# Turning the second activations of a quantised layer by DMA instead of on TensorE

## The reference

```python
def _act_quant(a):
    scale = QB / jnp.clip(jnp.max(jnp.abs(a), axis=-1, keepdims=True), 1e-05)
    return jnp.clip(jnp.round(a * scale), -QB, QB) / scale      # QB = 127
def _bitlinear(x, w):
    return jnp.einsum('bsd,od->bso', _act_quant(x), _weight_quant(w))
h = _rmsnorm(layernorm(x), norm_w)
value, gate = jnp.split(_bitlinear(h, w_gv), 2, axis=-1)        # 512 -> 2 x 2048
h = _bitlinear(value * jax.nn.silu(gate), w_out)                # 2048 -> 512
x = x + residual + h
```

## Time and profile before

| | |
|---|---|
| median of three executions | 1015.0 us |
| profiled execution, its time and span | 1013.59 us, 1011.6 us |
| TensorE busy, granted clock | 994.7 us (98%), 0.997 |
| VectorE, ScalarE, GpSimd busy | 676.1, 634.0, 354.8 us |
| quantised layer's tiles, first expand to last contract | about 238 to 437 us |

### The profile page before, as it was taken

The page is one execution under the profiler, slowest core; times in us unless marked ns, Lnnn a source line. Parts: engine busy times, 40 slices in busy tenths (PEclk is TensorE's granted clock), DMA queues, the critical chain, the costliest instruction groups (busy, mean ns, idle before and its releaser), DMA issues.

```text
span 1011.6 us, 15863 instructions
## 1 busy us (share of the span) xinstructions
PE 994.7 (98%) x5515; PEld 783.6 (77%) x5538; DVE 676.1 (67%) x1211; ACT 634.0 (63%) x950; POOL 354.8 (35%) x516
## 2 busy tenths in 40 slices
PE   9999999999999999999999999999999999999996
PEld 6887888886455555577877877888888999999996
DVE  6757555538999998768675755578625566666662
ACT  6776788746888899887666556121214466666662
POOL 1023222114655554146455445000100244445542
PEclk9999999999999999999999999999999999999998
DMA  6693666630200100121222333302053688888863
GB/s 233 246 332 117 180 185 193 178 87 22 85 22 23 30 24 1 48 78 42 84 84 84 136 115 99 115 1 84 14 197 117 224 242 228 226 229 252 243 155 46
DMA packets 48673, 128.96 MB, mean 127 GB/s; under 512 B 6368, under 2 KB 6368, under 8 KB 47840
## 3 DMA queue, kind: packets, MB, share of 16 engines
q1 hardware_dynamic: 37584, 99.54, 29.7%
q0 software_dynamic: 10448, 27.53, 11.8%
q10 hardware_dynamic: 576, 1.05, 0.3%
HBM read 99.79 MB, written 28.31 MB: 127 GB/s over the span
## 4 chain that ended last, share of the span: by engine, by line
PE 68%; DVE 2%; ACT 1%; issue 1%; POOL 1%; DVEq 0%; ACTq 0%; POOLq 0%
PE bank L60 16%; PE bank L61 16%; PE bank L62 16%; PE bank L1641 9%; PE bank L1662 5%; PE bank L2571 1%; PE bank L1653 1%; PE bank L1671 1%; PE bank L1737 1%; PE bank L1715 0%; PE bank L1716 0%; PE bank L2558 0%; PE bank L2541 0%; PE bank L1747 0%; PE bank L1748 0%
## 5 line engine op out<-in xcount | busy, mean ns | idle before, releaser
L1641 PE MATMUL bank<-w,f_qT 128*128 128x512 bf16 x496 | 115.9, 379 | 1.9 <-DVE f_h L1932 0.8
L2391 POOL DMA_INDIRECT out<-e_y,scatter_idx x32 | 69.0, 2157 | 109.5 <-ACT e_y L2500 89.6
L2374 POOL DMA_INDIRECT e_xg<-xn_rows,gather_idx x32 | 32.1, 1003 | 162.4 <-DVE gather_idx L2779 96.8
L1641 PEld LDWEIGHTS bank<-w,f_qT 128*128 128x128 bf16 x512 | 48.6, 98 | 51.6 <-issue 1.2
L2431 ACT ACTIVATE s_m_h<-s_mid 128x512 fp32r<-128x512 f32 (+1 forms) x24 | 15.2, 632 | 101.1 <-DVE s_mid L2789 55.2
L2898 DVE TENSOR_TENSOR e_mid<-bank,e_sil 128x256 f32<-128x256 f32 (+1 forms) x47 | 19.7, 420 | 59.2 <-ACT e_sil L2470 59.2
L1662 PE MATMUL bank<-w,f_q2T 128*128 128x512 bf16 x249 | 57.5, 379 | 1.2 <-ACT f_q2T L1324 0.8
L1932 DVE SCALAR_TENSOR_TENSOR f_h<-bank,f_columns,f_sg 128x512 f32<-128x512 f32 x64 | 47.9, 748 | 11.5 <-PE bank L1641 6.1
L60 PE MATMUL bank<-e_xT_h,e_wg_h 128*128 128x256 f32 (+1 forms) x192 | 55.1, 287 | 0.0
L61 PE MATMUL bank<-e_xT_l,e_wu_h 128*128 128x256 f32 (+1 forms) x192 | 54.1, 282 | 0.0
L62 PE MATMUL bank<-e_xT_h,e_wu_l 128*128 128x256 f32 (+1 forms) x192 | 54.0, 281 | 0.0
(11 more groups left out here) (481 smaller groups left out, 3274.9 us busy)
## 6 DMA issues: line engine op xcount, KB each, us to landing
wraw<-in_wffn SPq DMA_DIRECT2D x48, 512.0 KB, 4.2
e_raw_g<-in_ew_gate SPq DMA_DIRECT2D x16, 704.0 KB, 4.2
e_raw_u<-in_ew_up SPq DMA_DIRECT2D x16, 704.0 KB, 5.7
e_raw_d<-in_ew_down SPq DMA_DIRECT2D x16, 512.0 KB, 6.5
sorted_y<-e_y SPq DMA_DIRECT2D x19, 256.0 KB, 4.1
x_rows<-rows SPq DMA_DIRECT2D x16, 256.0 KB, 2.0
xn_rows<-a_work SPq DMA_DIRECT2D x16, 256.0 KB, 2.0
s_raw<-x_rows SPq DMA_DIRECT2D x16, 256.0 KB, 2.8
```

The costliest lines, as they stand in the source:

```text
L1641: ins = pe.matmul(bank[c % 2][:, :], qT[t % 2][:, k * P:(k + 1) * P], w_gv(k, col + c * 512), start=(k == 0), stop=(k == KD - 1))
L2374: gp.indirect_dma_start(xg[t][u][:, :], None, g.xn_dram, bass.IndirectOffsetOnAxis(g.gather_idx[:, slot:slot + 1], 0)).then_inc(e_arrived[ ...
L2391: gp.indirect_dma_start(io["out"], bass.IndirectOffsetOnAxis(g.scatter_idx[:, slot:slot + 1], 0), e_y[t][u][:, :], None, compute_op=ALU.ad ...
```

## The change

SyncE turns q2 with one transposing DMA per tile, SBUF to SBUF (128 x 2048 in bf16, 512 KB), for tiles 0 to 14, and with two of half the width for tile 15. TensorE's turn_q2, ScalarE's copy_q2T and the semaphores q2T_ready and q2T_copied are gone; contract waits for q2T_in, and for tile 15's second half for q2T_last. low moves from VectorE to ScalarE, ahead of high, for the tiles 1 to 14. low and high wait for the DMA of the tile before, which reads q2. On SyncE, renewed, the Wq, router and bias loads and turn_q2(0) now come before the summaries; the Wg load is behind turn_q2(14), the halves of tile 15 behind the Wg load. In TensorE's tail turn_x(14) comes before contract(15).

```diff
-        vbank, gbank, tbank, obank, sbank = g.bank[0:2], g.bank[2:4], [x[:, :].bitcast(bf16) for x in g.bank[4:6]], g.bank[6], g.bank[7]
+        vbank, gbank, obank, sbank = g.bank[0:2], g.bank[2:4], g.bank[6], g.bank[7]
         sbank_b = sbank[:, :].bitcast(bf16)
...
+                def turn_q2(t):
+                    sp.wait_ge(q2_low, t + 1)
+                    sp.wait_ge(q2_high, t + 1)
+                    if t:
+                        sp.wait_ge(o_ready, t)
+                    sp.dma_start(q2T[:, :].rearrange("p (k n) -> p k n", n=P), q2[:, :], transpose=True).then_inc(q2T_in, 16)
+
+                def turn_q2_half(n):
+                    sp.wait_ge((q2_low, q2_high)[n], TT)
+                    if n == 0:
+                        sp.wait_ge(o_ready, TT - 1)
+                    sp.dma_start(q2T[:, half(n)].rearrange("p (k n) -> p k n", n=P), q2[:, half(n)], transpose=True).then_inc((q2T_in, q2T_last)[n], 16)
+
                 sp.dma_start(norm_b[:, :], io["norm_w"][0, :].partition_broadcast(P)).then_inc(norm_in, 16)
-                for part, (ready, mine) in enumerate(((summ_hi, c_summ_h), (summ_lo, c_summ_l))):
-                    sp.wait_ge(ready, 1)
-                    sp.dma_start(g.summ_dram[B - 1, part, :, :], f(mine[:, :])).then_inc(summ_out, 16)
                 sp.wait_ge(renewed, 1)
...
                 sp.dma_start(bg_raw[:, :], io["bg"]).then_inc(bias_in, 16)
+                turn_q2(0)
+                for part, (ready, mine) in enumerate(((summ_hi, c_summ_h), (summ_lo, c_summ_l))):
+                    sp.wait_ge(ready, 1)
+                    sp.dma_start(g.summ_dram[B - 1, part, :, :], f(mine[:, :])).then_inc(summ_out, 16)
+                for t in range(1, TT - 1):
+                    turn_q2(t)
                 sp.wait_ge(norm_in, 16)
                 sp.wait_ge(summ_out, 32)
-                sp.wait_ge(q2_low, TT - 1)
-                sp.wait_ge(q2_high, TT - 1)
                 weights(1, io["wg"])
+                turn_q2_half(0)
+                turn_q2_half(1)
                 sp.wait_ge(w_lo, FIRST[1])
...
+                def low(t):
+                    act.wait_ge(h2_scaled, 2 * t + 1)
+                    act.wait_ge(q2T_in, 16 * t)
+                    act.activation(q2[:, half(0)], h2[t % 2][:, half(0)], ACT.Copy, bias=-MAGIC).then_inc(q2_low, 1)
+
                 def high(t):
...
                     if t:
-                        act.wait_ge(q2T_ready, 2 * t)
+                        act.wait_ge(q2T_in, 16 * t)
                     act.activation(q2[:, half(1)], h2[t % 2][:, half(1)], ACT.Copy, bias=-MAGIC).then_inc(q2_high, 1)
-
-                def copy_q2T(t, n):
-                    act.wait_ge(q2T_ready, 2 * t + n + 1)
-                    if t:
-                        act.wait_ge(o_ready, t)
-                    act.activation(q2T[:, half(n)], tbank[n][:, :], ACT.Copy).then_inc(q2T_copied, 1)
...
                 for i in range(TT):
-                    if have(i - 2):
-                        copy_q2T(i - 2, 0)
                     silu(i, 0)
...
                         split_x(i - 3)
-                    if have(i - 2):
-                        copy_q2T(i - 2, 1)
                     if i > 1 and have(i + 1):
...
                     if i > 1:
+                        low(i - 1)
                         high(i - 1)
...
                         normalise(i - 2)
-                copy_q2T(TT - 2, 0)
-                copy_q2T(TT - 2, 1)
                 act.wait_ge(renewed, 1)
...
                 high(TT - 1)
-                copy_q2T(TT - 1, 0)
-                copy_q2T(TT - 1, 1)
                 normalise(TT - 2)
...
-                def turn_q2(t):
-                    for n, ready in enumerate((q2_low, q2_high)):
-                        pe.wait_ge(ready, t + 1)
-                        if t == 0:
-                            pe.wait_ge(summ_ready, 1)
-                        if t:
-                            pe.wait_ge(q2T_copied, 2 * t + n - 1)
-                        for k in range(8):
-                            col = (8 * n + k) * P
-                            ins = pe.transpose(tbank[n][:, k * P:(k + 1) * P], q2[:, col:col + P], g.ident_b[:, :])
-                        ins.then_inc(q2T_ready, 1)
-
                 def contract(t):
...
                     for k in range(HID // P):
-                        if k % 8 == 0:
-                            pe.wait_ge(q2T_copied, 2 * t + k // 8 + 1)
+                        if k == 0:
+                            pe.wait_ge(q2T_in, 16 * (t + 1))
+                        if k == 8 and t == TT - 1:
+                            pe.wait_ge(q2T_last, 16)
                         ins = pe.matmul(obank[:, :], q2T[:, k * P:(k + 1) * P], w_out[:, k, :], start=(k == 0), stop=(k == HID // P - 1))
...
                         pe.wait_ge(h2_ready, 4 * TT)
-                    elif n == 2:
-                        pe.wait_ge(q2T_copied, 2 * TT)
                     if c == 0:
...
                     expand(i, 3)
-                    if have(i - 1):
-                        turn_q2(i - 1)
                 turn_x(TT - 3)
...
                 query(0)
-                turn_q2(TT - 1)
                 query(1)
+                turn_x(TT - 2)
                 contract(TT - 1)
-                turn_x(TT - 2)
                 query(2)
...
                     if t:
-                        v.wait_ge(q2T_ready, 2 * t - 1)
+                        v.wait_ge(q2T_in, 16 * t)
                     v.tensor_scalar(q2[:, half(0)], h2[t % 2][:, half(0)], MAGIC, None, ALU.subtract).then_inc(q2_low, 1)
...
                         split_summary()
-                    if have(i - 1):
-                        low(i - 1)
+                    if i == 1:
+                        low(0)
                     if i == 1:
...
                         weigh(3)
```

More of the change, by code:

```diff
@@ L994, in ffn0_to_experts1 @@
         am2_ready, amax2_ready, qs2_ready, deq2_ready = [sem(n) for n in "am2_ready amax2_ready qs2_ready deq2_ready".split()]
-        h2_scaled, q2_low, q2_high, q2T_ready, q2T_copied = [sem(n) for n in "h2_scaled q2_low q2_high q2T_ready q2T_copied".split()]
+        h2_scaled, q2_low, q2_high, q2T_in, q2T_last = [sem(n) for n in "h2_scaled q2_low q2_high q2T_in q2T_last".split()]
         o_ready, x2_ready, stats2_ready, mv2_ready, pool_post, shift2_ready = [
```

## The result

| | before | after |
|---|---|---|
| median of four executions | 1015.33 us | 1002.59 us |
| ratio, 95% interval | | 0.9888, 0.987 to 0.9906 |
| profiled execution: time, span | 1013.59, 1011.6 us | 1002.28, 1000.0 us |
| granted TensorE clock | 0.997 | 0.997 |

The account below looks back on a forecast made before the run. TensorE was taken to bound the kernel, busy 994.7 of 1011.6 us. Head -1.7, loop -10.1 and tail +0.6 summed to -11.2 us, giving a forecast of 1003.5 us, range 1000 to 1050.

Parts of the forecast that it names:

- the tile: Quantised layer, TensorE: a tile without its 16 transposes takes 11.91 - 0.89 = 11.02 us.
- the 0.05 a tile allowed back for order stalls: Order within a tile: product(i,2) ends about 0.1 us before it is wanted; 0.05 us a tile allowed for misses.
- L: Time from q2 complete until TensorE sees q2T: taken as 5 us, hidden up to 6.6 us.
- The two bounds (2.1 and 27): Estimated ends for the time from q2 complete to TensorE seeing q2T: 2.1 us and 27 us.
- rival B: Transposing DMA path longer than 8.4 us, so DMA and contraction alternate; 1049 to about 1320 us; chance 0.26.
- The piece count of 2048: Transposing DMA of q2: one piece per partition and 128-column block, 2048 pieces, 128 per engine, 1.6 us.
- both pages: Trainium skill on transposing DMAs: one gives 350 to 400 GB/s, the other 1309 ns per 128 x 128 block.
- the head: Tiles 0 and 1 of the layer: contract(1) at 270.1 in place of 271.81, -1.7 us.
- the 0.85 us wait at 267.92 ... shrinks: Head, TensorE: the wait for a product late on VectorE partly through low shrinks from 0.85 us.
- the tail: Layer's end after contract(13): contract(15) ends at 437.85 instead of 437.1 to 437.3; +0.6 us.
- loop: Twelve tiles between head and tail: 0.89 us less each, 0.05 allowed back, -10.1 us.
- Rival A: DMA path of 6.6 to 8 us, or ScalarE's order costing more, leaves part of the gain; chance 0.17.

Follow-up runs that it names:

- summ_later: The changed kernel with ScalarE's copy c_summ_h moved from ahead of quantise(3) to behind silu(2,1): 1001.95 us, ratio 0.9874 to the kernel before.
- four pieces: The changed kernel with q2T written by four transposing DMAs per tile instead of one (tiles 0 to 14): 1014.58 us, ratio 1.0012 to the kernel before.
- six: The changed kernel with q2T written by six transposing DMAs per tile instead of one: 1042.04 us, ratio 1.0276 to the kernel before.
- eight pieces: The changed kernel with q2T written by eight transposing DMAs per tile instead of one (tiles 0 to 14): 1095.04 us, ratio 1.0796 to the kernel before.

## Why the prediction was right, point by point

- **Right: the tile.** 11.02 us by subtraction of the transposes' place (0.89, not the listed 1.06), and 11.02 measured. 12 x 0.89 gave 10.7; the 0.05 a tile allowed back for order stalls was not needed. Putting 16 transposes back costs the whole gain, so this term is shown, not argued. product(i,2) ends at 344.61 in the tile shown and is wanted at 344.9: 0.3 us in hand, not 0.1.
- **Right: L.** Taken 5, measured 4.4; the room taken as 6.6 is 6.8. The half-width transfers took 3.1 from issue. The two bounds (2.1 and 27) were far apart, and the value nearest to the plain transfer held; nothing in the trace of before could tell it from the longer ones, so this choice was in part luck. One reading behind rival B was wrong: 597 ns is the longest plain issue of the earlier trace rows, not of the trace, where the load of Wo held SyncE's queue for 1.30 us at 432.89. The piece count of 2048 also held: a window of 5 us around one transfer shows 2080 packets under 512 B and a share of 55.2%, so 0.552 x 16 x 5 us / 2080 = 21.2 ns each, against the 12.3 estimated.

```profile
GB/s 0 0 0 0 0 0 0 0 0 27 188 225 217 217 217 199 199 229 223 215 213 207 219 231 223 207 182 195 223 124 15 0 0 0 0 0 0 0 0 0
DMA packets 2080, 0.52 MB, mean 105 GB/s; under 512 B 2080, under 2 KB 2080, under 8 KB 2080
...
q1 hardware_dynamic: 2080, 0.52, 55.2%
```

- The trace bears on both pages. While data flow, the slices show 180 to 230 GB/s. This is below the 350 to 400 GB/s of the Trainium skill, "Advanced Engine Details and Errata", X-Bar Transpose (TRN2). And 16 blocks take 4.2 us in one DMA. This is not 16 times the 1309 ns that the Trainium skill, "VectorE: DVE Perf Modes", The three transpose paths, has for one.
- **Wrong: the head.** -1.7 predicted, -0.16 came by the starts of contract(1), -0.36 in the stretch that the 1.7 was reckoned for. The failed step is "the 0.85 us wait at 267.92 ... shrinks": the sum even puts it at nothing, since 262.55 + 0.22 + 3.46 + 3.89 is 270.1. It grew to 1.85. I had put the product's lateness down to VectorE, where low left. The runs show that the product comes hardly earlier in the changed kernel (266.87 against 267.05): ScalarE is held behind c_summ_h's wait for GpSimd, and once that is gone VectorE's queue holds it. So the 0.89 us of turn_q2(1) turned into waiting. `summ_later` gives 0.7 of it back; low's new place accounts for 0.1.
- **Wrong in size: the tail.** +0.6 predicted, -0.7 came. contract(14) started 8.49 us after contract(13), not 9.23, as L was shorter than 5. The halves of tile 15 each landed 3.1 us after their issue, 1.3 apart, both within 4.5 us of the first issue and not 5.3, and so by the time contract(15) was due: it follows turn_x(14) without a wait for a DMA, and turn_x(14) waits for normalise alone:

```profile
421.91 0.66 PE L1669 MATMUL bank<-ident,f_xn 128*128 128x128 f32 x4 [0.43 <-ACT f_xn L1345]
422.62 3.40 PE L1660 MATMUL bank<-w,f_q2T 128*128 128x512 bf16 x15
```

- The errors of head (+1.5, of which 0.2 is from ahead of its stretch: 0.64 lost, 0.44 won), tail (-1.3) and loop (-0.6) nearly cancel, so the sum (-11.2, measured -11.6) is better than its parts. That is luck.
- **Rival A** did not occur in the loop, but the order is as tight as it said: with low on VectorE a tile takes 11.13. **Rival B** was real and near: it needs L = 8.4, and four pieces already reach 7.9, six 9.0. The price that I gave it was too low where the wait is long: at L = 11.4 it gives 1015 + 56 = 1071, and eight pieces took 1095, since the clock falls as well.

## What to carry to other kernels

Where TensorE bounds a stage and the DMA engines lie idle, one transposing DMA per tile took transposes and their copies out at no cost here. It can do so as long as the time from the data's completion to their use has room for issue and landing; count that room beforehand, from starts in the timeline. Issue one large transposing DMA, not many pieces: here 2 were free, 4 took the whole gain and 8 made the kernel 80 us slower than before. Look also for other DMAs that start in the same moment: four pieces were hidden in the tiles without a gather. Where a wait at the layer's head hangs on another engine, TensorE's saved time only lengthens it. Subtract a group's place in the pipe (0.89 us), not its listed length (1.06), then check that the next engine (here ScalarE) is relieved too.

## What the runs showed of the hardware

- A transposing DMA held SyncE's queue longer than most plain ones: 1.2 to 1.3 us for 256 to 1024 columns of 128 partitions, 1.9 for 2048, against 0.32 to 0.60 for the plain issues of the earlier trace rows. A few plain ones took as long, the load of Wo before 1.30. Issue to landing was 4.2 us for 2048 columns, 3.1 for 1024, 2.4 for 512. Back to back they follow at 1.29 us.
- The last of four pieces reached TensorE 3.8 to 4.2 us after its issue in the usual tiles with a gather of f_x (in one of them, the gather was issued at 339.6 and the last piece at 339.7), and 2.6 in a tile without, contract(14)'s. One DMA of the same 512 columns alone landed after 2.4. The pieces' packets themselves were through 5.9 us after the first issue, both in most tiles with a gather and in those without. The gather's packets follow right behind them; how they hold the completion back is not shown.
- After an idle time of 3.95 us TensorE was granted 0.50 of its clock for the first 2.5 us of the following contraction and 0.63 on average over the rest (6.07 us in place of 3.6). With six pieces a contraction took 3.61 us after an idle 1.93, and 5.30 after an idle 2.37.
